# Gathers of a graph network: POOL waits for each slot itself, with unrolled turns and fixed index columns

## The reference

```python
h = relu(layernorm(x))
h = gcn(h, src, dst, ones, W1, b1)            # norm, gather h[src], sum by dst
h = h / max(norm(h), 1e-12)
ev = sigmoid(concat(h[src], h[dst]) @ We1 + be1)
na = relu(segment_sum(ev * h[src], dst) @ Wn1 + bn1)
ev2 = sigmoid(concat(na[src], na[dst]) @ We2 + be2)
g = relu(segment_sum(ev2 * na[src], dst) @ Wn1 + bn1)
out = x + gcn(g, src, dst, ev2, W2, b2)       # weights ev2
```

## Time and profile before

| | |
|---|---|
| median of 3 runs | 6434.93 us |
| span of the profiled execution | 6459.6 us |
| POOL busy | 3296.7 us (51%) |
| PE busy | 2679.0 us (41%) |
| DVE busy | 2411.2 us (37%) |
| ACT busy | 903.4 us (14%) |
| bytes moved by DMA | 366.86 MB, mean 57 GB/s |

### The profile page before, as it was taken

One profiled execution on the slowest core, in us unless ns is written; L12 is line 12 of the kernel. 1 busy time (PEld: TensorE's weight loads), 2 busy tenths in 40 slices (PEclk: granted clock), 3 DMA queues, 4 the chain that ended last, 5 costly groups with the idle time before them and its releaser, 6 DMA issues. The chain is left out here.

```text
span 6459.6 us, 78329 instructions
## 1 busy us (share of the span) xinstructions
PE 2679.0 (41%) x8018; PEld 1804.9 (28%) x8019; DVE 2411.2 (37%) x8424; ACT 903.4 (14%) x2361; POOL 3296.7 (51%) x3528
## 2 busy tenths in 40 slices
PE   1333333346444444344464444443345343433443
PEld 1322322334232222222242222222223233322332
DVE  4333333335333333333353333333344333333334
ACT  4000000003222222222231121211123000000000
POOL 6555555554544544444444544444443555555555
PEclk8555555557666666666676666666667555555555
DMA  3111111112222222222222222222222111111111
GB/s 95 40 38 40 40 37 40 40 41 69 75 67 66 69 64 66 71 66 66 59 88 64 70 62 66 69 63 65 66 65 81 45 37 38 40 36 39 39 40 52
DMA packets 236072, 366.86 MB, mean 57 GB/s; under 512 B 118303, under 2 KB 151923, under 8 KB 236020
## 3 DMA queue, kind: packets, MB, share of 16 engines
q0 software_dynamic: 134912, 332.75, 18.6%
q1 hardware_dynamic: 97522, 32.56, 2.1%
q10 hardware_dynamic: 3618, 1.35, 0.1%
HBM read 342.12 MB, written 23.49 MB: 57 GB/s over the span
## 5 line engine op out<-in xcount | busy, mean ns | idle before, releaser
L441 POOL DMA_INDIRECT rows<-table,idx_ring x3328 | 3153.6, 948 | 2978.3 <-SPq L348 1969.3
L736 PE MATMUL ps<-rows,weights 128*128 x7040 | 2493.5, 503 | 3630.1 <-issue 1516.5
L736 PEld LDWEIGHTS ps<-rows,weights 128*128 128x128 f32 x7040 | 1658.2, 283 | 4465.4 <-issue 4328.0
L1034 DVE TENSOR_TENSOR acc<-acc,ps 128x128 f32 (+2 forms) x3520 | 1251.1, 355 | 2546.2 <-issue 1750.2
L629 ACT ACTIVATE step<-xbuf,rows 128x128 f32 x1760 | 653.1, 400 | 2226.4 <-issue 1068.2
L1021 DVE SCALAR_TENSOR_TENSOR weights<-iota,pair_dst,step 128x128 f32<-128x128 f32 x880 | 305.4, 349 | 409.8 <-issue 351.9
L1018 DVE SCALAR_TENSOR_TENSOR weights<-iota,pair_dst,step 128x128 f32<-128x128 f32 x880 | 301.1, 348 | 399.4 <-issue 317.9
L1024 DVE TENSOR_SCALAR weights<-iota,pair_dst,gate 128x128 f32<-128x128 f32 x880 | 307.6, 361 | 271.5 <-issue 250.1
L1016 DVE TENSOR_SCALAR weights<-iota,pair_dst 128x128 f32<-128x128 f32 x880 | 256.0, 299 | 297.8 <-issue 268.2
L581 ACT ACTIVATE rows<-ps 128x128 f32<-128x128 f32 x49 | 13.6, 278 | 1403.5 <-PE ps L772 1402.9
L629 ACT ACT_TABLE_LOAD x55 | 70.6, 1283 | 356.6 <-issue 223.7
(11 more groups left out here) (134 smaller groups left out, 574.6 us busy)
## 6 DMA issues: line engine op xcount, KB each, us to landing
rows<-table,idx_ring POOLq DMA_INDIRECT x3328
table<-tab SPq DMA_DIRECT2D x12, 903.0 KB, 4.7
idx_ring<-edge_src SPq DMA_DIRECT2D x418, 4.0 KB
table<-acc SPq DMA_DIRECT2D x13, 448.0 KB, 3.0
out_nodes<-acc SPq DMA_DIRECT2D x6, 448.0 KB
table<-tab SPq DMA_DIRECT2D x2, 516.0 KB, 4.3
acc<-dst_s,lb_idx POOLq DMA_INDIRECT x49
table<-tab SPq DMA_DIRECT2D x2, 387.0 KB, 4.0
```

The costliest lines, as they stand in the source:

```text
L441: nc.gpsimd.indirect_dma_start(rows[:, u, 0:row_floats[k]], None, tables[k], bass.IndirectOffsetOnAxis(ap=idx_ring[:, u:u + 1], axis=0)).t ...
L736: nc.tensor.matmul(ps[u % W_RING][:, 0:WIDTH[k]], weights[:, u % W_RING, :], rows[:, bass.ds(slots[u], 1), 0:WIDTH[k]].rearrange("p o f -> ...
L1034: nc.vector.tensor_tensor(sums, sums, ps[u % W_RING][:, 0:WIDTH[k]], ALU.add).then_inc(pairs_added, 1)
```

## The change

POOL no longer loops over turns and halves; its 52 turns are written out, so each gather reads a fixed column of `edge_src`. The ring `idx_ring`, SP's staging DMAs, and the semaphores between SP and POOL are gone. POOL loads the sixteen entries that it needs for a turn itself and, from the second turn of a pass on, waits on `pairs_done` ahead of each gather; the wait is followed by an increment of `slot_freed`, for which nothing waits. SP keeps the relay of landed tiles alone. POOL waits once for the setup of `edge_src` and for the entries before its first pass. ACT's copy of sixteen columns behind the last gathered one is gone, so two thresholds on `setup_moved` fall by one.

```diff
             def relay_pass(k):
-                sp.wait_ge(entry_ready, 1)
+
                 with sp.Fori(0, GATHER_TURNS) as i:
-                    for h in range(2):
-                        _, (entered,) = nc.values_load_multi_w_load_instructions(
-                            entry_row[0:1, bass.ds(i * UNROLL + h * HALF, 1)], engines=[SYN], min_val=0, max_val=PAIRS,
-                            skip_runtime_bounds_check_because="entries are bounded when they are made")
-                        for u in range(h * HALF, (h + 1) * HALF):
-
-                            sp.wait_ge(landed[u], i * 16 + 16 * (GATHER_TURNS * k + 1))
-                            sp.sem_inc(tiles_landed, 1)
-                            if u == h * HALF + HALF // 2 - 1:
-
-
-                                sp.wait_ge(pairs_done, entered + (PAIRS * k + W_RING))
-                                sp.sem_inc(half_free, 1)
-                                sp.wait_ge(idx_staged[1 - h], i * 16 + 16 * (GATHER_TURNS * k + 1 + h))
-                                sp.sem_inc(half_ready[1 - h], 1)
-
-                        stage(i + 1, h)
+                    for u in range(UNROLL):
+
+                        sp.wait_ge(landed[u], i * 16 + 16 * (GATHER_TURNS * k + 1))
+                        sp.sem_inc(tiles_landed, 1)
...
                 pool.wait_ge(tab_stored[k], 16 * (NODE_TURNS if k == 0 else len(PIECES)))
-                with pool.Fori(0, GATHER_TURNS) as i:
-                    for h in range(2):
-
-                        pool.wait_ge(half_ready[h], i + (GATHER_TURNS * k + 1))
-                        pool.sem_inc(half_begun, 1)
-                        for u in range(h * HALF, (h + 1) * HALF):
-                            nc.gpsimd.indirect_dma_start(rows[:, u, 0:row_floats[k]], None, tables[k],
-                                                         bass.IndirectOffsetOnAxis(ap=idx_ring[:, u:u + 1], axis=0)).then_inc(landed[u], 16)
+                for i in range(GATHER_TURNS):
+                    if i > 0:
+                        entered = nc.values_load_multi_w_load_instructions(
+                            entry_row[0:1, (i - 1) * UNROLL + 1:i * UNROLL + 1], engines=[POO], min_val=0, max_val=PAIRS,
+                            skip_runtime_bounds_check_because="entries are bounded when they are made")[1]
+                    for u in range(UNROLL):
+                        if i > 0:
+
+                            pool.wait_ge(pairs_done, entered[u] + (PAIRS * k + W_RING))
+                            pool.sem_inc(slot_freed, 1)
+                        nc.gpsimd.indirect_dma_start(rows[:, u, 0:row_floats[k]], None, tables[k],
+                                                     bass.IndirectOffsetOnAxis(ap=edge_src[:, i * UNROLL + u:i * UNROLL + u + 1], axis=0)).then_inc(landed[u], 16)
...
+            pool.wait_ge(setup_moved, 2)
+            pool.wait_ge(entry_ready, 1)
             gather_pass(0)
...
-            act.activation(edge_src[:, GATHERED:GATHERED + UNROLL], ps[4][:, 0:UNROLL], ACT.Copy).then_inc(setup_moved, 1)
```

More of the change, by code:

```diff
@@ L26 @@
 UNROLL = 16
-HALF = UNROLL // 2
 GATHER_TURNS = -(-EDGE_TILES // UNROLL)
@@ L31 @@
 PAIRS = TURNS * UNROLL
-BLOCKS = -(-max(PAIRS, GATHERED + UNROLL) // PART)
+BLOCKS = -(-max(PAIRS, GATHERED) // PART)
 TABLE = BLOCKS * PART
@@ L135, in gnn_kernel @@
         credit = sb("credit", [PART, 9])
-        idx_ring = sb("idx_ring", [PART, UNROLL], u32)
         rows = sb("rows", [PART, UNROLL, ROW])
@@ L210, in gnn_kernel @@
             sem(n) for n in ("w1T_sent", "w1T_ready", "b1_rep_ready", "w_prod", "w_prod_ready"))
-        idx_staged, half_ready = ([sem(f"{n}{h}") for h in range(2)] for n in ("idx_staged", "half_ready"))
-        half_free, half_begun = sem("half_free"), sem("half_begun")
+        slot_freed = sem("slot_freed")
         landed, tiles_landed = [sem(f"landed{u}") for u in range(UNROLL)], sem("tiles_landed")
@@ L308, in _ @@
             sp.dma_start(pair_row[0:1, :, :], pair_rows[:, :]).then_inc(ld_pair_row, 16)
[L310 to L316, removed]
-            for h in range(2):
-                stage(0, h)
-            sp.wait_ge(idx_staged[0], 16)
-            sp.sem_inc(half_ready[0], 1)
             def store(k, tab, lo, n):
@@ L705, in _ @@
             pe.wait_ge(ld_w, 16 * 13)
-            pe.wait_ge(setup_moved, 5)
+            pe.wait_ge(setup_moved, 4)
             for c in range(2):
@@ L994, in _ @@
             v.wait_ge(ld_pair_row, 16)
-            v.wait_ge(setup_moved, 5)
+            v.wait_ge(setup_moved, 4)
             nc.vector.memset(tab2[:, :, ONE:ONE + 1], 1.0)
```

## The result

The changed kernel takes 5852.8 us (median of four runs, 5819.2 to 5871.4) where the kernel before takes 6436.9 us beside it: a ratio of 0.907, 95% interval 0.903 to 0.912. The forecast was 6303 us with 5980 as its lower end, so the direction was right and the size far too small. The span fell from 6459.6 to 5869.6 us, and the four passes account for it: 5492.8 us together, against the 6081.0 of the earlier trace rows.

The account below looks back on a forecast made before the run. The prediction took the kernel as bound by a seesaw between POOL's gather bursts and slowed consumers. -302 + 90 + 80 = -132 us on the 6459.6 us span gave 6327.6, less 24.7 for the runs' median 6303 us; range 5980 to 7000.

Parts of the forecast that it names:

- the stretch: Time during gathers when sequencer instructions of SP and DVE take 700 ns; said to end 4.2 us after the last gather's start.
- the seesaw: Between POOL and consumers: while gathers fly, consumers run fast, then crawl; POOL fills its ring and stops, and consumers empty it.
- Slots freed one by one: POOL's slot waits: shorter pauses and bursts save 82 us in passes without gates and 220 with them, -302 us.
- the line: Gather bursts: n tiles take 1.80n - 2.3 us without gates, 2.20n - 2.9 with, drawn through bursts of sixteen and eight.
- Late gathers: POOL's gathers released by pairs finished inside the slow stretch prolong it: +90 us, at most 238 in passes with gates.
- the trickle: Rival at gathers released inside the slow stretch: it feeds itself, +255 us without gates, +350 with, about 7040; chance in full 0.18.
- Instructions: Sequencers: net 15 more a turn, the load of 16 values on POOL at 1.10 us the largest; +80 us of at most 260.
- The relay and SP's stagings: On SP: removed staging DMAs and a shorter instruction list save at most 2 x 0.49 us a turn, 204 us.
- Faster still: Rival at POOL's pauses: shorter than allowed, cheap like the trace's bursts of eight, -414 us, about 6020; chance 0.13.
- POOL's instructions slowed: Rival: POOL's added sequencer instructions take 0.70 us each, 2.1 us a gather, +2830 us if fully exposed; chance 0.07 (over 7400).
- P: Theory of the experiments, not the prediction: POOL's 3.59 us load is the pause that ends the slow stretch once a turn.
- L: Theory of the experiments: POOL's long load is plain cost on its queue; shortening it gains up to 500 us.

Follow-up runs that it names:

- first set: Experiments on one chip with the changed kernel's three tables of pair numbers held as 16-bit instead of 32-bit integers; ratios are to the kernel before.
- third: Set of experiments with 32-bit tables and one AND more at each wait for a loaded number, on three chips; kernel before 6458.7, 6337.6 and 6345.4 us.
- halves: Changed kernel with one AND more per wait, POOL waiting once for eight slots on one-number loads: 6404.4 us, ratio 0.993; with 16-bit tables instead, without AND, 6703.7 us.
- aligned load: Changed kernel with one AND more per wait, POOL's load of sixteen numbers starting at a multiple of sixteen: 5797.3 us, ratio 0.898.
- the control: Changed kernel with only one AND more at each wait for a loaded number, 32-bit tables: 5830.9 us, ratio 0.920.
- quarters: Changed kernel with one AND more per wait, POOL waiting once for four slots on one-number loads: 5949.3 us, ratio 0.938.
- the first control: Changed kernel with its tables of pair numbers held as 16-bit instead of 32-bit integers: 6242.5 us, ratio 0.968.

## Why the prediction was wrong, step by step

*What bounds the kernel: right where the stretch exists, and now measured.* On four chips without slow instructions the same kernel takes 4545 us. By that comparison the seesaw costs 1890 of 6435 us. I had read the stretch as a property of gathers under way. That isn't enough for it: all chips met ran the same gathers, and only some showed it. The result's runs, the chip of the first set and the three of the third had it; four others never did. No chip of the experiments was met twice, and the record names none for the result's runs, so whether it belongs to the chip or to what surrounds it at that hour is open.

*Slots freed one by one, -302 us: the main failure.* The measured price is 0.085 to 0.094 of the kernel before, 550 to 607 us (halves against the changed kernel and against the aligned load); 470 us if the control across chips is taken. The step that failed is the burst of the new kernel, found where a pause of 4.25 us beyond the cadence meets the line through two burst lengths: 7.5 tiles in 13.7 us with gates, 11.9 in 19.1 without. In place of such short cycles the slow stretches still come once in 14.6 tiles and 25.0 us with gates (15.1 tiles and 29.8 us before), and once in 16.0 tiles and 25.4 us without (15.7 and 26.4). The cycle kept its length in tiles and became shorter in time; more and shorter bursts are not what brought the gain. With gates the line is 2.20n - 2.9 us, 29.2 us for 14.6 tiles. A burst of eleven in pass 1 of the changed kernel, and where the next one starts:
```profile
1920.73 0.94 POOL L417 DMA_INDIRECT rows<-table,edge_src  x1 [2.10 <-issue]
...
1933.24 0.95 POOL L417 DMA_INDIRECT rows<-table,edge_src  x1 [0.30 <-issue]
1939.27 0.94 POOL L417 DMA_INDIRECT rows<-table,edge_src  x1 [5.09 <-PE ps L713]
```
That is 18.5 us, where the line says 21.3. Without gates, twelve from 706.33 to 722.83 take 16.5 us for the line's 19.3, and ten from 727.06 to 741.00 take 13.9 for 15.7, both up to a single late gather. Nor does the length of a burst alone set its time: bursts of twelve in pass 1 take 17.0 us up to the next gather in the changed kernel (9 of them), and 21.5 us in the quarters (45 of them, another chip). Both points of the line came from bursts after which POOL stood until a whole half was free; that their time held the waiting of the old rule, and the slope charged it to every tile, is my reading of this and isn't shown by a run of its own. The pauses went otherwise too. I had 4.25 us beyond the cadence of 1.25 us. The gathers came in 561 groups, 203 of them a single gather, and the pauses between groups were 2.1 to 2.6 us beyond the cadence on average. The 4.24 us from 722.83 to 727.06 look like the forecast by luck alone: they are the whole distance, and POOL's load made them.

*Late gathers, +90: not refuted; the trickle, 0.18: did not occur.* The trickle would have lengthened the slow stretches, and they fell by 572 us in all. The late gather of 722.83 was followed by additions of 40 ns from 725.0 on, 2.2 us after it, where I had taken each gather to hold the slow stretch open for 4.2 us. But over the whole trace, the 81 stretches with one late gather in them ended 4.6 us (median) after the last gather of their burst, and the 124 without one 3.2 us. If the late gather did that, it is some 110 us in all, near the +90. A stretch that lasts longer also has more room for a late gather, so this doesn't show the cause.

*Instructions, +80: too high, and for the wrong reason.* 32 register operations more a turn cost 0 to 80 us, so the 15 net of the change 0 to 37 us by the same measure (the pages count 2564 instructions more, 12 a turn). The load was the larger item and I had its length wrong by a factor of three, because the row I took was of a load at a multiple of sixteen, and the change's begins one beyond it.
The Trainium skill (Runtime: NRT & Kernel Launch, Instruction fetch mechanics) puts a TENSOR_LOAD at about 200 ns a register, by which sixteen are an estimated 3.2 us; the changed kernel's 3.59 us is near it, and I had said that the trace contradicts the page. The runs show both: 1.05 to 1.10 us from 32-bit numbers at a multiple of sixteen, 3.59 us one number further, 3.4 to 3.8 us from 16-bit numbers. I should have asked why row and page differ.
What the longer load costs is small all the same (34 to 140 us by the two ways of counting above, across chips). On three other engines at once, ahead of each turn of pairs, it was dear (the first control).

*The relay and SP's stagings, at most 204 in the other direction: not exceeded, but wrong in kind.* With eight slots kept, their removal gave 54 us. But with single slots and 16-bit tables SP's wait for pairs costs 152 us, because it holds up the tiles behind it. I listed SP's L346 as POOL's releaser and never asked who else was queued behind it on SP; ACT's 572.2 us at L341 were in the same view. The staging alone was measured only where nothing is slow (4537.0 against 4535.2 us), so its part on the other chips is open.

*Faster still, 0.13.* Its 6020 us was the nearest of the stated cases, and still 167 us too high, as it was built on the eights of the same line.

*POOL's instructions slowed, 0.07: seldom, and hidden.* The additions of L415 ran at a median of 32 ns; 21 of them and 16 of POOL's waits took 600 to 900 ns. With one AND more (the control of the third set) 704 of POOL's additions and ANDs and 322 of its waits did, so POOL is not exempt as L435 and L439 had made me think. The gathers between which they fell still came every 1.25 us, as from 129.8 to 148.6 in that control. All additions of L415 in the changed kernel:
```profile
L415 POOLq ALU_OP  x3264: 13/32/1410, 130.7 to 5832.8; - x192
```
My upper bound, in which every instruction more is paid for by all, was 260 us for 15 a turn, so some 550 for the 32 of the AND, which cost at most 80: that price did not come. The Trainium skill (NOTIFIC — the notification-queue block, Overflow: three behaviours) says that inside the block its pipeline holds back rather than lose a record; no run shows the block.

*The sum.* -132 us against -590 on the span. The -302 were also summed wrongly: I set the new cost against 1.656 in both passes without gates and against 1.946 in both with them, where each pass's own cost gives 47 + 77 + 110 + 155 = 389 us from the same line. The four pass times that I wrote at the end (1350, 1530, 1570, 1370) add up to 5820 us, 129 less than the sum's own 6081 - 132; they go with the 389 and most of the two positive terms. They missed by 33, 118, 135 and 42 us: the passes with gates by most.

*Open:* what makes a chip show the stretch; how much of the 590 us each of its two parts, finer freeing and relay, holds when both act (the relay with staging and loop 54 at eight slots, SP's wait 152 at single slots); by what steps finer freeing shortens the slow stretches; what the staging alone costs where they exist; why four short loads cost 147 us in the first set, since neither P nor L gives it.

## What to carry to other kernels

Where a ring is refilled by an engine that can run ahead, free it slot by slot: one, four and eight slots to a wait gave 0.898, 0.938 and 0.993 of the kernel before here, on the chips where bursts of gathers slow the other engines, and made no difference where they don't. A wait on a queue is paid by everything behind it, so list for each wait of a relay who else that queue serves before pricing its removal. Don't extrapolate a rate from bursts whose pauses were made by the rule that the change takes away; count over the whole trace before one turn is read as the rule; and take a load's price from a row of the same type and the same alignment. A time from one chip can hold an effect that the next chip lacks: ratios of 0.907 and 0.998 are the same change.

The best version measured is the change with the aligned load: 5797.3 us where the kernel before takes 6458.7, and 4535.4 where that takes 4544.8.

## What the runs showed of the hardware

- Two kinds of chip, or of hour: register instructions of DVE, SP, ACT and PE and waits of DVE, SP and PE at some 700 ns in stretches that mostly begin 2 to 8 us into a burst of gathers (kernel before 6338 to 6459 us on those chips), or never (40 and 17 ns in all 6848 records of two lines, 4545 us).
- A load of sixteen registers: 1.05 to 1.10 us from 32-bit numbers at a multiple of sixteen, 3.59 us one number further, 3.4 to 3.8 us from 16-bit numbers. One register 0.27 to 0.29 us, four 0.93 us.
- Slow stretches ended a median of 4.1 us after the start of the burst's last gather in the kernel before (216 of them) and 3.2 us in the changed kernel where no late gather fell into them (124); with one late gather 4.6 us after the burst's last and 2.1 us after the late one (81).
